# Cross-attention on one core: the output projection's quarters spread over the batches

## The chip, the cores and the metric

The kernel runs on one core of one Trainium2 chip. The metric is device time in microseconds (us) of one execution, lower is better. The core has a matrix engine (TensorE, PE in the rows, with its weight loads as PEld), VectorE (DVE), ScalarE (ACT), GpSimd (POOL) and SyncE (SP), which here only issues DMAs. Each runs its own instruction queue in order, and they wait for each other by semaphores.

## What is computed

32 batches of 56 queries attend to 1500 context rows each, with 32 heads of 16 dimensions. The context serves as keys and as values. Cut to what matters, the reference is:

```python
x = layernorm(hidden) * ln_gamma + ln_beta          # hidden: 32 x 56 x 512
Q = split_heads(x @ Wq.T)                            # 32 heads of 16
K = V = split_heads(ctx)                             # 32 x 1500 x 512
scores = einsum('bhsd,bhtd->bhst', Q, K) / 4
probs = softmax(where(mask, scores, -inf))
attn = einsum('bhst,bhtd->bhsd', probs, V).transpose(0, 2, 1, 3).reshape(B, S, 512)
return hidden + attn @ Wout.T
```

## The kernel before

The layer norm and the query projection of all batches come first (about the first 100 us). Then the main loop runs over 32 batches, and in each over 12 slots of 125 context rows. Slot k of a batch is one round of an attention pipeline, written out by hand on every engine.

- TensorE lays the negated row maxima into four PSUM banks (L266, `begin_scores`), adds the scores of all heads (L274, `score_blocks`), and later multiplies the slot before's exponentials with the values (L289, `times_values`). The four score banks are not doubled: L266 of slot k+1 waits for ScalarE's exponential of slot k.
- ScalarE takes the exponential of the whole slot in one instruction (L370, 125 x 1792 elements). There is one of them per slot, so its starts are the clock by which this document measures: slot k's length is the time from its start to that of slot k+1.
- To have the row maxima before the scores, TensorE also computes bfloat16 scores of a batch ahead: 48 tiles a batch, four a slot (L234, `score_tile`). VectorE adds the mask to each and takes its maximum (L335). These tiles pass through a ring of two PSUM banks: a tile may be written when the one two places before it in the ring has been taken. In a slot the first tile stands before L266; here it is called the lead tile. The second and third stand behind the scores, and the fourth behind the values.
- GpSimd adds the exponentials of every four slots (L422), and TensorE sums those over the context rows with a matrix of ones (L303, `add_denominators`). It does this in slots 6 and 7, 10 and 11, and in 2 and 3 of the next batch. VectorE inverts the sums in four reciprocals, one in slot 3 and three in slot 4 (`INVERT_AT`, L359), and GpSimd divides the heads by them (L435, `divide_heads`) into `attnT`, behind the third of its additions.
- Slot 10 also turns the maxima of the next batch (L242), for which VectorE first reduces them (L344).
- Two batches make a pair with 112 query rows. When the second batch of a pair is divided, the output projection of the pair is due: `project_out` (L251), in four quarters of 128 columns. Each quarter is a unit of the same ring of two PSUM banks; VectorE adds the residual (L352, `add_residual`) into `result`, from `x_res`, which SyncE loads (L208) before and stores (L212) after.

`OUT_AT` names where the quarters stand, as (batch of the pair after, slot). Each stands at the end of its slot, behind the fourth tile and ahead of the next slot's lead tile:

```python
OUT_AT = [(0, 8), (0, 9), (1, 0), (1, 1)]
```

The two engines' ends of the loop over slots read, on TensorE and on VectorE:

```python
                    if tiles:
                        score_tile(pe, tiles[3])
                    for unit in slot_others(b, k):
                        project_out(pe, unit)
```

So before the change a pair's quarters stand in slots 8 and 9 of the next even batch, and 0 and 1 of the odd batch behind it. `result`, `x_res` and `attnT` exist once each. The last pair's four quarters stand behind the loop.

Of the kernel before, what the change touches and what calls it, by code (L numbers as in the profile page):

```python
# [20 lines left out]
PAIR_Q = 2 * QUERIES  # L21
# [11 lines left out]
ROWS_SLOT = 10  # L33
OUT_PARTS = 4
OUT_COLS = HIDDEN // OUT_PARTS
OUT_AT = [(0, 8), (0, 9), (1, 0), (1, 1)]
TOKENS = BATCH * QUERIES

UNIT_TILES = [1, 3, 4, 4, 4]
# [15 lines left out]

def slot_others(b, k):

    return [("out", b // 2 - 1, OUT_AT.index((b % 2, k)))] if (b % 2, k) in OUT_AT and b > 1 else []

FIRST_TILES = [("tile", 0, t) for t in range(MAX_TILES)] + [("tile", 1, t) for t in range(AHEAD)]
RING = FIRST_TILES[:]
RING += [unit for b in range(BATCH) for k in range(SLOTS) for unit in slot_tiles(b, k) + slot_others(b, k)]
RING += [("out", BATCH // 2 - 1, part) for part in range(OUT_PARTS)]
RING_AT = {unit: n for n, unit in enumerate(RING)}


def build(nc, x, kt, ctx, mask_lanes, mask_rows, wq_t, wout_t, gamma, beta, out):
    with ExitStack() as stack:  # L70
        def sb(name, shape, dt=F32):
            return stack.enter_context(nc.sbuf_tensor(name, shape, dt))
# [20 lines left out]
        den_inv = sb("den_inv", [128, BLOCKS, QUERIES])  # L93
        own = sb("own", [128, 2, BLOCKS, QUERIES])
        heads = sb("heads", [128, BLOCKS, QUERIES])
        attnT = sb("attnT", [128, BLOCKS, PAIR_Q])
        x_res = sb("x_res", [128, HIDDEN])
        result = sb("result", [128, HIDDEN])
        ident = sb("ident", [128, 128])
# [80 lines left out]
        def filled_past(unit):  # L180
            return RING_AT[unit] + 1
# [63 lines left out]
        def project_out(pe, unit):  # L245

            _, d, part = unit
            bank = ring_bank(pe, unit)
            pe.wait_ge(attn_ready, 2 * d + 2)
            for g in range(BLOCKS):  # L250
                mm = nc.tensor.matmul(bank[0:PAIR_Q, 0:OUT_COLS], attnT[:, g, :],  # L251
                                      woutT[:, g, OUT_COLS * part:OUT_COLS * (part + 1)],
                                      start=(g == 0), stop=(g == BLOCKS - 1))
            mm.then_inc(ring_filled, 1)
# [68 lines left out]
        def take_unit(dve, unit):  # L323
            dve.wait_ge(ring_filled, filled_past(unit))
            if unit[0] == "tile":
                take_tile(dve, unit[1], unit[2], bank_of(unit))
            else:
                add_residual(dve, unit[1], unit[2], bank_of(unit))
# [99 lines left out]

        def divide_heads(pool, b):
            pool.wait_ge(den_taken, BLOCKS * (b + 1))  # L430
            if b % 2 == 0 and b > 0:
                pool.wait_ge(ring_filled, filled_past(("out", b // 2 - 1, OUT_PARTS - 1)))
            pool.wait_ge(heads_added, b + 1)
            at = QUERIES * (b % 2)
            nc.gpsimd.tensor_tensor(attnT[:, :, at:at + QUERIES], heads[:], den_inv[:], ALU.mult).then_inc(attn_ready, 1)  # L435

        end = BATCH - 1
        block = stack.enter_context(nc.Block())
# [2 lines left out]
        def _(sp):  # L441
# [30 lines left out]
            for b in range(BATCH):  # L472
                if b > 0:
                    if b < end:
                        sp.wait_ge(pv_done, SLOTS * b)
                        load_k(sp, b + 1, 2)
                    sp.wait_ge(pv_done, SLOTS * b)
                    load_v(sp, b, 2)
                if b < end:
                    sp.wait_ge(pv_done, SLOTS * b + CHUNK)  # L480
                    if b + 2 < BATCH:
                        load_k(sp, b + 2, 0)
                    load_v(sp, b + 1, 0)
                    if b + 2 < BATCH:
                        wait_taken(sp, ("tile", b, MAX_TILES - 1))
                        load_mask(sp, b + 2)
                if b % 2 == 1:
                    if b > 1:
                        store_result(sp, b // 2 - 1)
                    load_residual(sp, b // 2)  # L490
                if b + 2 < BATCH:
                    sp.wait_ge(pv_done, SLOTS * b + 2 * CHUNK)
                    load_k(sp, b + 2, 1)
                if b < end:
                    sp.wait_ge(pv_done, SLOTS * b + 2 * CHUNK)
# [54 lines left out]
        def _(dve):  # L550
# [52 lines left out]
                        take_unit(dve, unit)  # L603
            for g in range(BLOCKS):
                invert_denominators(dve, end, g)
            for part in range(OUT_PARTS):
                take_unit(dve, ("out", BATCH // 2 - 1, part))

        @block.scalar
        def _(act):  # L610
# [32 lines left out]
        def _(pe):  # L643
# [58 lines left out]
            pe.wait_ge(exped, BATCH * SLOTS)  # L702
            times_values(pe, end, SLOTS - 1)
            last_denominators(pe)
            for part in range(OUT_PARTS):
                project_out(pe, ("out", BATCH // 2 - 1, part))

# [41 lines left out]
```

## Time and profile before

| what | us |
|---|---|
| median of 3 runs (lowest, highest) | 1474.55 (1472.51, 1477.33) |
| the profiled execution: its time | 1475.04 |
| the profiled execution: its span, first to last instruction | 1473.3 |
| TensorE matmuls busy in the span | 1391.1 (94%) |
| GpSimd busy | 1242.8 (84%) |
| VectorE busy | 1072.2 (73%) |
| ScalarE busy | 751.6 (51%) |

A busy share is an average over all slots and says what an engine does, not who waits for whom. The mean granted TensorE clock is 0.992 of full speed. The rows further down are read by the start times of one kind of instruction, or by who stands behind whom inside a single slot.

### The profile page before, as it was taken

Reading aid. Unit: us, or ns where it says so; the run is one execution under the profiler, and the core shown is the slowest. Engines: PE = TensorE matmul, PEld = TensorE weight load, DVE = VectorE, ACT = ScalarE, POOL = GpSimd, SP = SyncE. Lnnn points to the kernel's source line nnn. Section 1 sums busy time; section 2 is a strip of 40 time slices with the busy share of each in tenths; the row PEclk is TensorE's granted clock in tenths of the full one; section 3 lists DMA queues with packets and bytes.
Section 4 is the critical chain, followed back from the end, with each engine's and each line's share of the span. In section 5 each row is a group of like instructions: output and inputs, shape, how many; then the busy total and the mean of one; then the engine's idle time right before and its main releaser. Section 6 shows DMA issues by size and latency. Waiting matters only on the chain.

```text
span 1473.3 us, 66063 instructions
## 1 busy us (share of the span) xinstructions
PE 1391.1 (94%) x30000; PEld 992.9 (67%) x30000; DVE 1072.2 (73%) x3356; ACT 751.6 (51%) x623; POOL 1242.8 (84%) x434
## 2 busy tenths in 40 slices
PE   6999999999999999999999999999999999999986
PEld 4337677676766767676676767676676767677675
DVE  6657777777777777777777777777777777777730
ACT  2125555555555555545555555554555555555553
POOL 1009998989999898989989898998989899898986
PEclk9999999999999999999999999999999999999999
DMA  9303444435444443444444444444344443444320
GB/s 296 80 38 141 176 165 146 171 135 183 158 166 166 148 171 141 174 161 156 176 164 152 155 156 166 172 151 166 149 160 158 162 171 148 175 159 152 147 86 8
DMA packets 39161, 224.90 MB, mean 153 GB/s; under 512 B 4546, under 2 KB 4578, under 8 KB 26882
## 3 DMA queue, kind: packets, MB, share of 16 engines
q1 hardware_dynamic: 38882, 220.68, 41.3%
q8 instruction: 236, 3.87, 1.1%
q14 instruction: 43, 0.35, 0.1%
HBM read 216.90 MB, written 3.77 MB: 150 GB/s over the span
## 4 chain that ended last, share of the span: by engine, by line
PE 68%; DVE 24%; ACT 4%; issue 3%; POOL 1%; DMA 0%; ACTq 0%; SPq 0%; POOLq 0%; DVEq 0%
PE ps L234 20%; DVE masked L335 18%; PE ps L289 17%; PE ps L274 12%; PE ps L303 6%; PE ps L251 5%; PE ps L266 4%; PE ps L664 4%; ACT probs L370 3%; DVE den_inv L359 3%; PE ps L242 1%; POOL sums L422 1%; DVE tile_max L335 1%; DVE stats L555 0%; DVE probs L572 0%
## 5 line engine op out<-in xcount | busy, mean ns | idle before, releaser
L335 DVE CUSTOM_DVE_ANT_0 masked<-ps,mask_tile 112x500 bf16<-112x500 f32 x1536 | 974.9, 672 | 310.1 <-PE ps L234 295.5
L370 ACT ACTIVATE probs<-ps,mask_bias 125x1792 f32<-125x1792 f32 x384 | 674.2, 1756 | 629.3 <-PE ps L274 607.1
L422 POOL TENSOR_TENSOR sums<-sums,probs 125x1792 f32<-125x1792 f32 x191 | 763.5, 3997 | 10.1
L422 POOL TENSOR_TENSOR sums<-probs 125x1792 f32<-125x1792 f32 x96 | 383.7, 3997 | 197.3 <-ACT probs L370 197.3
L234 PE MATMUL ps<-kT,qdb 32*112 32x500 bf16 x1536 | 487.7, 414 | 43.8 <-DVE tile_max L335 41.4
L274 PEld LDWEIGHTS ps<-qd,kT 32*125 32x125 f32 x12288 | 433.9, 185 | 1.6 <-issue 0.3
L274 PE MATMUL ps<-qd,kT 32*125 32x112 f32 x12288 | 432.7, 269 | 2.4 <-issue 2.4
L289 PE MATMUL ps<-probs,v 125*32 125x112 f32 x12288 | 372.9, 262 | 1.2 <-ACT probs L370 0.7
L289 PEld LDWEIGHTS ps<-probs,v 125*32 125x32 f32 x12288 | 299.2, 110 | 68.7 <-issue 44.8
L234 PEld LDWEIGHTS ps<-kT,qdb 32*112 32x112 bf16 x1536 | 157.9, 123 | 245.6 <-DVE tile_max L335 184.0
L266 PE MATMUL ps<-max_rows,ones_row 4*125 4x448 bf16 x1536 | 189.6, 389 | 12.7 <-ACT probs L370 9.8
L335 DVE DVE_READ_ACCUMULATOR2_ANT tile_max<- 112x1 f32 x1536 | 128.0, 83 | 0.0
L303 PE MATMUL ps<-sums,ones 125*32 125x224 f32 x1520 | 111.3, 365 | 0.0
L266 PEld LDWEIGHTS ps<-max_rows,ones_row 4*125 4x125 bf16 x1536 | 60.1, 129 | 53.8 <-ACT probs L370 38.2
L359 DVE RECIPROCAL den_inv<-ps 128x56 f32<-128x56 f32 x128 | 63.5, 500 | 34.2 <-PE ps L316 29.4
L251 PE MATMUL ps<-woutT,attnT 128*112 128x128 f32 x512 | 73.0, 288 | 5.0 <-POOL attnT L435 2.6
L251 PEld LDWEIGHTS ps<-woutT,attnT 128*112 128x112 f32 x512 | 60.8, 181 | 21.2 <-DVE tile_max L335 11.4
L664 PE MATMUL ps<-sums,v 128*128 128x448 f32 (+2 forms) x160 | 65.7, 530 | 3.1 <-DMA v<-in_wq_t 1.4
L303 PEld LDWEIGHTS ps<-sums,ones 125*32 125x32 f32 x1520 | 29.9, 108 | 43.0 <-issue 42.1
L352 DVE TENSOR_TENSOR result<-ps,x_res 112x128 f32<-112x128 f32 x64 | 18.7, 292 | 43.6 <-PE ps L251 43.6
L626 ACT COPY qT<-ps 128x448 f32<-128x448 f32 (+2 forms) x20 | 9.1, 457 | 63.5 <-PE ps L664 63.4
L664 PEld LDWEIGHTS ps<-sums,v 128*128 128x128 f32 x160 | 27.1, 212 | 18.8 <-issue 12.5
(49 smaller groups left out, 254.6 us busy)
## 6 DMA issues: line engine op xcount, KB each, us to landing
kT<-in_kt SPq DMA_DIRECT2D x96, 1000.0 KB, 5.2
v<-in_ctx SPq DMA_DIRECT2D x96, 1000.0 KB
mask_tile<-mask_add SPq DMA_DIRECT2D x32, 328.1 KB, 13.6
x_res<-in_x SPq DMA_DIRECT2D x16, 224.0 KB, 14.1
out<-result SPq DMA_DIRECT2D x16, 224.0 KB, 14.1
probs<-in_x SPq DMA_DIRECT2D x14, 224.0 KB, 9.2
v<-in_wq_t SPq DMA_DIRECT2D x1, 1024.0 KB, 5.9
woutT<-in_wout_t SPq DMA_DIRECT2D x1, 1024.0 KB, 20.7
```

The lines of the kernel that those rows point to most:

```text
L234: nc.tensor.matmul(bank[0:PAIR_Q, 0:KEYS], qdb[rows, b % 2, g, :], keys, start=True, stop=True).then_inc(ring_filled, 1)
L251: mm = nc.tensor.matmul(bank[0:PAIR_Q, 0:OUT_COLS], attnT[:, g, :], woutT[:, g, OUT_COLS * part:OUT_COLS * (part + 1)], start=(g == 0), st ...
L266: nc.tensor.matmul(ps[0:LANES, r, 0:BANK_Q], ones_row[rows, :], max_rows[rows, b % 2].rearrange("p g n -> p (g n)"), start=True, stop=Fals ...
L274: mm = nc.tensor.matmul(ps[0:LANES, r, PAIR_Q * g:PAIR_Q * (g + 1)], kT[rows, b % 2, k // CHUNK, g, k % CHUNK, :], qd[rows, b % 2, g, :], ...
L289: mm = nc.tensor.matmul(acc[ROW * r:ROW * (r + 1), g, :], v[0:LANES, c, k % CHUNK, col:col + ROW], probs[0:LANES, k % PROBS, r, PAIR_Q * g ...
L303: mm = nc.tensor.matmul(den[ROW * r:ROW * (r + 1), :, :], ones[0:LANES, e, :], own_q, start=(j == 0 and e == 0), stop=(j == SUMS - 1 and e ...
L335: nc.vector.tensor_tensor_reduce(out=masked[0:PAIR_Q, t % 2, :], in0=bank[0:PAIR_Q, 0:KEYS], in1=mask_tile[0:PAIR_Q, b % 2, KEYS * c:KEYS ...
L352: nc.vector.tensor_tensor(result[0:PAIR_Q, cols], bank[0:PAIR_Q, 0:OUT_COLS], x_res[0:PAIR_Q, cols], ALU.add).then_inc(ring_taken, 1)
L359: nc.vector.reciprocal(den_inv[:, g], den[:, g]).then_inc(den_taken, 1)
L370: nc.scalar.activation(probs[0:LANES, k % PROBS], ps[0:LANES, 0:TILES_R, 0:BANK_Q], ACT.Exp, bias=mask_bias[0:LANES, n:n + 1], scale=SCALE ...
L422: nc.gpsimd.tensor_tensor(total, before, probs[0:LANES, slot % PROBS], ALU.add).then_inc(summed, 1)
L664: mm = nc.tensor.matmul(bank, wqT[:, h, 128 * c:128 * (c + 1)], xT[u % 2][:, h, 0:w], start=(h == 0), stop=(h == BLOCKS - 1))
```

## The change

A pair's quarters move to (batch of the pair after, slot) (0, 9), (1, 3), (1, 9) and (2, 3), so that every batch from 3 on has one in slot 3 and one in slot 9. They now reach into the batches in which the next pair is divided, so `attnT` is doubled. SyncE's store of `result` and load of `x_res` move from the odd batches to the even ones. Of the last two pairs five quarters are left behind the loop, not four, and among them the store of the last pair but one and the load of the last residual. The diff, without what only follows from the new index of `attnT`:

```diff
-OUT_AT = [(0, 8), (0, 9), (1, 0), (1, 1)]
+OUT_AT = [(2, 9), (3, 3), (3, 9), (4, 3)]
...
 def slot_others(b, k):
-    return [("out", b // 2 - 1, OUT_AT.index((b % 2, k)))] if (b % 2, k) in OUT_AT and b > 1 else []
+    return [("out", (b - after) // 2, part) for part, (after, slot) in enumerate(OUT_AT)
+            if slot == k and after % 2 == b % 2 and b >= after]
...
-RING += [("out", BATCH // 2 - 1, part) for part in range(OUT_PARTS)]
+LAST_OUTS = [("out", d, part) for d in range(BATCH // 2 - 2, BATCH // 2) for part in range(OUT_PARTS)]
+LAST_OUTS = [unit for unit in LAST_OUTS if unit not in RING]
+RING += LAST_OUTS
...
-        attnT = sb("attnT", [128, BLOCKS, PAIR_Q])
+        attnT = sb("attnT", [128, 2, BLOCKS, PAIR_Q])
...
-            if b % 2 == 0 and b > 0:
-                pool.wait_ge(ring_filled, filled_past(("out", b // 2 - 1, OUT_PARTS - 1)))
+            if b % 2 == 0 and b > 2:
+                pool.wait_ge(ring_filled, filled_past(("out", b // 2 - 2, OUT_PARTS - 1)))
...
-                if b % 2 == 1:
-                    if b > 1:
-                        store_result(sp, b // 2 - 1)
-                    load_residual(sp, b // 2)
+                if b % 2 == 0:
+                    if b > 2:
+                        store_result(sp, b // 2 - 2)
+                    if b > 0:
+                        load_residual(sp, b // 2 - 1)
...
+            store_result(sp, BATCH // 2 - 2)
+            load_residual(sp, BATCH // 2 - 1)
             store_result(sp, BATCH // 2 - 1)
```

TensorE before the change, batch 2, from the values of slot 8 to the start of slot 10's scores (L234 is a tile, L251 a quarter, L289 the values, L266 and L274 the next slot's scores):

```order
L289 MATMUL ps<-probs,v 32x112 x16
L234 MATMUL ps<-kT,qdb 112x500
L251 MATMUL ps<-woutT,attnT 112x128 x4
L234 MATMUL ps<-kT,qdb 112x500
L266 MATMUL ps<-max_rows,ones_row 125x448 x4
L274 MATMUL ps<-qd,kT 125x112 x16
L234 MATMUL ps<-kT,qdb 112x500 x2
L289 MATMUL ps<-probs,v 32x112 x16
L234 MATMUL ps<-kT,qdb 112x500
L251 MATMUL ps<-woutT,attnT 112x128 x4
L234 MATMUL ps<-kT,qdb 112x500
L266 MATMUL ps<-max_rows,ones_row 125x448 x4
```

TensorE after the change, the same place (the line numbers are 3 higher):

```order
L292 MATMUL ps<-probs,v 32x112 x16
L237 MATMUL ps<-kT,qdb 112x500 x2
L269 MATMUL ps<-max_rows,ones_row 125x448 x4
L277 MATMUL ps<-qd,kT 125x112 x16
L237 MATMUL ps<-kT,qdb 112x500 x2
L292 MATMUL ps<-probs,v 32x112 x16
L237 MATMUL ps<-kT,qdb 112x500
L254 MATMUL ps<-woutT,attnT 112x128 x4
L237 MATMUL ps<-kT,qdb 112x500
L269 MATMUL ps<-max_rows,ones_row 125x448 x4
L277 MATMUL ps<-qd,kT 125x112 x16
L237 MATMUL ps<-kT,qdb 112x500 x2
```

The quarter of slot 8 is gone, and that of slot 9 stands where it stood.

VectorE before the change, batch 3, from the end of slot 3's last tile to the middle of slot 4 (L335 a tile in two instructions, L359 a reciprocal):

```order
L335 ISA tile_max 112x1
L359 RECIPROCAL den_inv<-ps 128x56
L335 ISA masked,tile_max<-ps,mask_tile 112x500
L335 ISA tile_max 112x1
L359 RECIPROCAL den_inv<-ps 128x56
L335 ISA masked,tile_max<-ps,mask_tile 112x500
L335 ISA tile_max 112x1
L335 ISA masked,tile_max<-ps,mask_tile 112x500
L335 ISA tile_max 112x1
L359 RECIPROCAL den_inv<-ps 128x56
```

VectorE after the change, the same place:

```order
L338 ISA tile_max 112x1
L362 RECIPROCAL den_inv<-ps 128x56
L355 TENSOR_TENSOR result<-ps,x_res 112x128
L338 ISA masked,tile_max<-ps,mask_tile 112x500
L338 ISA tile_max 112x1
L362 RECIPROCAL den_inv<-ps 128x56
L338 ISA masked,tile_max<-ps,mask_tile 112x500
L338 ISA tile_max 112x1
L338 ISA masked,tile_max<-ps,mask_tile 112x500
L338 ISA tile_max 112x1
L362 RECIPROCAL den_inv<-ps 128x56
```

The residual addition of a quarter now stands between slot 3's reciprocal and slot 4's lead tile. On TensorE the quarter stands in slot 3 in the same way, behind the fourth tile.

SyncE before the change, an even batch from its slot 4 on and the odd one behind it up to its slot 4:

```order
L195 DMA kT<-in_kt 128x2000
L199 DMA v<-in_ctx 125x2048
L202 DMA mask_tile<-mask_add 112x1500
L195 DMA kT<-in_kt 128x2000
L199 DMA v<-in_ctx 125x2048
L195 DMA kT<-in_kt 128x2000
L199 DMA v<-in_ctx 125x2048
L195 DMA kT<-in_kt 128x2000
L199 DMA v<-in_ctx 125x2048
L202 DMA mask_tile<-mask_add 112x1500
L212 DMA out<-result 112x512
L208 DMA x_res<-in_x 112x512
```

SyncE after the change, the same place:

```order
L198 DMA kT<-in_kt 128x2000
L202 DMA v<-in_ctx 125x2048
L205 DMA mask_tile<-mask_add 112x1500
L215 DMA out<-result 112x512
L211 DMA x_res<-in_x 112x512
L198 DMA kT<-in_kt 128x2000
L202 DMA v<-in_ctx 125x2048
L198 DMA kT<-in_kt 128x2000
L202 DMA v<-in_ctx 125x2048
L198 DMA kT<-in_kt 128x2000
L202 DMA v<-in_ctx 125x2048
L205 DMA mask_tile<-mask_add 112x1500
```

The store and the load of the residual moved from behind the mask of the odd batch to behind that of the even batch.

## Rows read from the trace of the kernel before

Times are us from the span's start. A row of a timeline is start, duration, engine, line, operation, tiles, count, and in brackets the idle time ahead of it with what ended it.

**Rows 1.** The page, part 4: the chain that ended last, by engine.
```profile
PE 68%; DVE 24%; ACT 4%; issue 3%; POOL 1%; DMA 0%; ACTq 0%; SPq 0%; POOLq 0%; DVEq 0%
```

**Rows 2.** Timeline of ScalarE, batches 13 and 14: start, duration, line, tiles, wait.
```profile
654.61 1.75 ACT L370 ACTIVATE probs<-ps,mask_bias 125x1792 f32<-125x1792 f32 x1 [1.68 <-PE ps L274]
...
663.10 1.76 ACT L370 ACTIVATE probs<-ps,mask_bias 125x1792 f32<-125x1792 f32 x1 [2.27 <-PE ps L274]
...
669.65 1.76 ACT L370 ACTIVATE probs<-ps,mask_bias 125x1792 f32<-125x1792 f32 x1 [1.56 <-PE ps L274]
...
683.14 1.76 ACT L370 ACTIVATE probs<-ps,mask_bias 125x1792 f32<-125x1792 f32 x1 [1.68 <-PE ps L274]
...
689.62 1.75 ACT L370 ACTIVATE probs<-ps,mask_bias 125x1792 f32<-125x1792 f32 x1 [1.48 <-PE ps L274]
...
697.17 1.76 ACT L370 ACTIVATE probs<-ps,mask_bias 125x1792 f32<-125x1792 f32 x1 [1.68 <-PE ps L274]
...
706.88 1.75 ACT L370 ACTIVATE probs<-ps,mask_bias 125x1792 f32<-125x1792 f32 x1 [1.48 <-PE ps L274]
710.20 1.75 ACT L370 ACTIVATE probs<-ps,mask_bias 125x1792 f32<-125x1792 f32 x1 [1.56 <-PE ps L274]
713.87 1.75 ACT L370 ACTIVATE probs<-ps,mask_bias 125x1792 f32<-125x1792 f32 x1 [1.92 <-PE ps L274]
...
723.93 1.76 ACT L370 ACTIVATE probs<-ps,mask_bias 125x1792 f32<-125x1792 f32 x1 [1.68 <-PE ps L274]
728.39 1.76 ACT L370 ACTIVATE probs<-ps,mask_bias 125x1792 f32<-125x1792 f32 x1 [2.71 <-PE ps L274]
732.42 1.76 ACT L370 ACTIVATE probs<-ps,mask_bias 125x1792 f32<-125x1792 f32 x1 [2.27 <-PE ps L274]
...
739.46 1.76 ACT L370 ACTIVATE probs<-ps,mask_bias 125x1792 f32<-125x1792 f32 x1 [1.68 <-PE ps L274]
```

**Rows 3.** Timeline of TensorE, batch 14, slot 8 into 9 and 10.
```profile
725.33 0.42 PE L234 MATMUL ps<-kT,qdb 32*112 32x500 bf16 x1
725.69 1.13 PE L251 MATMUL ps<-woutT,attnT 128*112 128x128 f32 x8
726.74 0.42 PE L234 MATMUL ps<-kT,qdb 32*112 32x500 bf16 x1
...
729.20 0.42 PE L234 MATMUL ps<-kT,qdb 32*112 32x500 bf16 x1
...
732.20 0.42 PE L234 MATMUL ps<-kT,qdb 32*112 32x500 bf16 x1
```

**Rows 4.** Timeline of TensorE, batch 13, slot 9 and start of slot 10.
```profile
687.61 0.69 PE L234 MATMUL ps<-kT,qdb 32*112 32x500 bf16 x2
...
689.91 0.42 PE L234 MATMUL ps<-kT,qdb 32*112 32x500 bf16 x1 [0.24 <-DVE tile_max L335]
```

**Rows 5.** Timeline of TensorE, batch 14, end of slot 3, start of 4.
```profile
708.51 0.42 PE L234 MATMUL ps<-kT,qdb 32*112 32x500 bf16 x2
...
710.67 0.42 PE L234 MATMUL ps<-kT,qdb 32*112 32x500 bf16 x1 [0.40 <-DVE tile_max L335]
```

**Rows 6.** Timeline of the SyncE queue, batch 14, slot 4.
```profile
712.82 0.44 SPq L202 DMA_DIRECT2D mask_tile<-mask_add  x1
```

**Rows 7.** DMA times to landing by tile: of x_res.
```profile
DMA to landing us min/median/max: 6.3/14.1/14.8
```

**Rows 8.** The same of out (from result).
```profile
DMA to landing us min/median/max: 2.3/14.1/14.5
```

**Rows 9.** Timeline of all engines, batch 31 and the end.
```profile
1432.91 0.41 PE L266 MATMUL ps<-max_rows,ones_row 4*125 4x448 bf16 x4 [0.78 <-ACT probs L370]
...
1464.12 0.66 POOL L435 TENSOR_TENSOR attnT<-heads,den_inv 128x224 f32<-128x224 f32 x1 [2.61 <-DVE den_inv L359]
...
1464.92 5.39 PE L251 MATMUL ps<-woutT,attnT 128*112 128x128 f32 x32 [2.61 <-POOL attnT L435]
```

**Rows 10.** Windows at the end: busy us (instructions) by engine, granted clock, DMA.
```profile
1466.00:1470.00 4.00, 4.00 (x24) 4.00 (x24) 0.88 (x3) 0.00 (x0) 0.00 (x0) 0.60 0.01 4
```

More of the change, by code:

```diff
@@ L250, in project_out @@
             for g in range(BLOCKS):
-                mm = nc.tensor.matmul(bank[0:PAIR_Q, 0:OUT_COLS], attnT[:, g, :],
+                mm = nc.tensor.matmul(bank[0:PAIR_Q, 0:OUT_COLS], attnT[:, d % 2, g, :],
                                       woutT[:, g, OUT_COLS * part:OUT_COLS * (part + 1)],
@@ L430, in divide_heads @@
             pool.wait_ge(den_taken, BLOCKS * (b + 1))
-            if b % 2 == 0 and b > 0:
-                pool.wait_ge(ring_filled, filled_past(("out", b // 2 - 1, OUT_PARTS - 1)))
+            if b % 2 == 0 and b > 2:
+                pool.wait_ge(ring_filled, filled_past(("out", b // 2 - 2, OUT_PARTS - 1)))
             pool.wait_ge(heads_added, b + 1)
             at = QUERIES * (b % 2)
-            nc.gpsimd.tensor_tensor(attnT[:, :, at:at + QUERIES], heads[:], den_inv[:], ALU.mult).then_inc(attn_ready, 1)
+            nc.gpsimd.tensor_tensor(attnT[:, b // 2 % 2, :, at:at + QUERIES], heads[:], den_inv[:], ALU.mult).then_inc(attn_ready, 1)
         end = BATCH - 1
@@ L605, in _ @@
                 invert_denominators(dve, end, g)
-            for part in range(OUT_PARTS):
-                take_unit(dve, ("out", BATCH // 2 - 1, part))
+            for unit in LAST_OUTS:
+                take_unit(dve, unit)
         @block.scalar
@@ L704, in _ @@
             last_denominators(pe)
-            for part in range(OUT_PARTS):
-                project_out(pe, ("out", BATCH // 2 - 1, part))
+            for unit in LAST_OUTS:
+                project_out(pe, unit)
 FILL_PLAN = [(kind, 0, c) for kind in ("x", "q") for c in range(BLOCKS)] + [("x", 1, c) for c in range(BLOCKS)]
```

## The prediction

> **What bounds the kernel now.** I read the chain that ended last first: 68% of it is TensorE, 24% VectorE, nothing on GpSimd or DMA that counts [rows 1]. TensorE is thus the engine to follow, but a share does not say what one more instruction costs in a given slot. For that I took the starts of the exponentials, one per slot, over an odd and an even batch in a row [rows 2]. Batch 13 lasts 697.17 - 654.61 = 42.56 us and batch 14 739.46 - 697.17 = 42.29, a pair 84.85.
>
> The reader is to see three kinds of slot in [rows 2]. Slots 0 to 2 of batch 14 take 9.71 together, 3.24 each, and so do batch 13's slots 8 and 9 (6.48). There an exponential takes 1.76, the next scores start behind it and need the other 1.48 (the bracket): the loop of ScalarE and the scores sets the pace, and TensorE has a little room. Slots with more TensorE work are longer: slot 3 takes 3.32. And a slot with a quarter takes 4.46 (batch 14, slot 8, 723.93 to 728.39), the next one with a quarter 4.03. In batch 13 slots 0 and 1 take 8.49, the same two costs.
>
> Inside such a slot the fourth tile starts at 725.33, the quarter at 725.69, the next lead tile at 726.74 [rows 3]: 1.41 from fourth tile to lead tile, and 728.39 - 726.74 = 1.65 more to the next exponential. Without a quarter the fourth and the lead tile start together [rows 5]. That gives me the rule that I use below: with a quarter, slot length = start of the fourth tile after the exponential + 1.41 + 1.65. For slot 8: 1.40 + 3.06 = 4.46.
>
> The last thing to see is what a quarter leaves behind. While TensorE does it, VectorE runs out of tiles and catches up. In slot 9 behind a quarter the fourth tile starts 0.81 after the exponential (729.20 - 728.39 [rows 2, 3]), in the ordinary slot 9 of batch 13 1.23 after (687.61, with the exponential 3.24 before 689.62 [rows 2, 4]). And in slot 10 the third tile starts 0.22 before the exponential when slot 9 had a quarter (732.20 against 732.42), but 0.29 after it, held by VectorE, when it had none (689.91 against 689.62 [rows 2 to 4]). The credit is worth 0.51: slots 10 and 11 take 7.04 in batch 14 and 7.55 in batch 13.
>
> **The change slot by slot.** Nothing is computed more or less: 64 quarters and 64 residual additions before and after. What changes is in which slot they fall, and what VectorE's rest is good for there.
>
> Slot 9, now in every batch, alone: fourth tile at 1.23, so 1.23 + 3.06 = 4.29. Against batch 13's 3.24 that is a cost of 1.05; against batch 14's 4.03 it is 0.26 more, since there the quarter before had paid for it. Its credit in slot 10 stays in even batches and is new in odd ones (-0.51).
>
> Slots 8, 0 and 1: the quarters leave. Slot 8 falls to 3.24 (-1.22 in even batches), slots 0 and 1 to 6.47 (-2.02 in odd ones). Slots 2 and 3 of batch 13 took 6.55 and those of batch 14 6.56, so the leaving itself takes nothing back there.
>
> Slot 3, now in every batch: the fourth tile starts at 708.51 - 706.88 = 1.63 [rows 2, 5], late already, because the denominators stand in this slot. With the quarter: 1.63 + 3.06 = 4.69, a cost of 1.37. This is the dear place. The credit comes in slot 4: there the third tile waits 0.40 for VectorE and starts 0.47 after the exponential [rows 5], since the reciprocal of slot 3 and the first of slot 4 stand ahead of it. With the quarter, the reciprocal of slot 3 runs beside it, and the third tile finds its bank free as in slot 9 behind a quarter. Slot 4 then is an ordinary 3.24 where it was 713.87 - 710.20 = 3.67. Slots 5 to 7 took 10.06 in batch 14, 0.35 over three ordinary ones, since VectorE enters them behind the other two reciprocals and TensorE meets its backlog in the denominator slots. It now enters a little earlier; I take 9.92, nearer to the row than to 9.71, so 13.16 for slots 4 to 7. They took 13.73 in batch 14 and 13.49 in batch 13 [rows 2], where the quarters of slots 0 and 1 had left VectorE a little ahead. The bounds are 12.95 and, if nothing is given back, 13.73.
>
> The new batch: 9.71 + 4.69 + 13.16 + 3.24 + 4.29 + 7.04 = 42.13. An even batch gains 0.16, an odd one 0.43. Thirteen even batches (4 to 28) and fourteen odd ones (3 to 29) give 2.1 + 6.0 = 8.1. Batch 2 only loses its quarter of slot 8 and keeps slot 9: 42.29 - 1.22 + 0.26, a gain of 1.0. In batch 30 I count 0.2 gained, as in any even one. Batch 31 has no tiles, so TensorE waits 0.78 for the exponential in slot 3 [rows 9] and a quarter of 1.13 [rows 3] costs 0.35 there; slot 9's is hidden, as slots 0 and 1 were. Together 9.0 gained in the loop.
>
> **Waits that move.** GpSimd's first exponential sum of a batch still waits for slot 1, and its third, behind which `attnT` is made, is done by slot 5; both `attnT` halves are free by then. SyncE issues the store and the residual load behind the mask, whose issue is at 712.82, 2.62 after slot 4's exponential [rows 2, 6]. After the change the values stand about 0.9 earlier in slot 4, so the mask goes out at 1.7, the store at 2.1, the load at 2.6 after it. The quarter of slot 9 is added some 2.7 after slot 9's exponential, which is 13.16 + 3.24 = 16.4 later than slot 4's. So the load has 16.5 us. It takes 14.1, at most 14.8 [rows 7], and the store 14.5 at most [rows 8]. Hidden, with 1.7 to spare. If that cover fails, VectorE waits in slot 9 with the lead tile of slot 10 queued behind it, and TensorE's third tile behind that.
>
> **The end.** Of five quarters the first needs only old heads: it runs between the last denominators and the division, a gap in which TensorE idles 2.61 [rows 9]; 1.13 fits. But its addition stands behind the last reciprocals (about 1464.1), so SyncE issues the store at about 1464.4 and the last residual at 1464.8. The additions wait for it, where before the first could run when its quarter was done, at 1464.92 + 1.13 = 1466.05 [rows 3, 9]. The landing costs between 2.3 (the last store, with nothing beside it [rows 8]) and 6.3 (the fastest residual [rows 7]). With 2.3 it is there at 1467.1, and the third quarter starts on its bank at 1467.4, when TensorE is still at the second: nothing lost. With 6.3 it is there at 1471.1, then two more quarters of 1.1 follow, some 3 us lost. The queue is empty as for the last store, so I take 2.8, and a loss of 0.3.
>
> The Trainium skill (DMA: Bandwidth & Descriptors, Anatomy of one DMA) gives about 2.0 us fixed and the bytes over 436 GB/s, though for GpSimd's path: an estimate of 2.5 us for 224 KB, near the lower row, and no loss at the end. No run here shows that path.
>
> Sum against the profiled execution: 1475.0 - 9.0 + 0.3 = 1466.3. It lies 0.5 above the median of the runs shown, so for the median I say 1465.8.
>
> **Rivals.** *Slot 10's credit fails in odd batches* (take_max stands between the residual addition and slot 10's lead tile; a lone quarter in slot 9 adds 0.26 later than the second of two). Then 14 x 0.51 = 7.1 is missing: 1472.9, about no change. For it: no row shows a lone quarter in slot 9. Against: its lead tile is later by the same 0.26.
>
> *Slot 3 gives nothing back* (the other side). The quarter puts its residual addition between two reciprocals, and VectorE's backlog stays: slots 4 to 7 take 13.73. The batch is 42.70; even batches lose 0.41 x 13, odd ones 0.14 x 14, together 7.3; batch 2 still gains 1.0, batches 30 and 31 and the end lose 1.1: 1474.55 + 7.4 = 1482. It decides from 13.47 for these four slots (8.9 over 28 batches is 0.31 each), where the gain is gone. Against it: the addition waits only for the quarter, and slot 4's wait of 0.40 is for tiles that the quarter lets VectorE finish.
>
> *The residual comes late.* A landing of over 16.5 costs its excess once a pair; 14 pairs at 1 us are 14 us, but the rows leave 1.7 us. At 17.2 the time is 1475.6.
>
> *The clock at the end.* In the last quarters the granted clock is 0.60 [rows 10], between the levels 1.2 and 2.4 GHz, after TensorE had idled twice. The extra quarter fills part of the second gap; if the clock stays full, at most 4.0 x 0.4 = 1.6 is saved: 1464.2. The Trainium skill (TensorE: Matmul & The Clock Gate, What's actually happening) has the throttled state as the default that activity releases, which speaks for it; whether so short a filling does it, no row here shows.
>
> **How the numbers follow.** My forecast 0.66; the clock beside it 0.08; slot 10's credit missing 0.14; slot 3 without credit 0.08; a late residual 0.04. Runs of one kernel lie some 2.5 us around their median, so 0.3% (4.4 us) is what can be told from no change. Faster: 0.66 + 0.08 = 0.74 and a little of the partial cases, 0.75. Slower 0.09, the rest 0.16. The range takes in the clock, slot 10's case and that spread: 1461 to 1473.5.
>
> **What would show it.** After: slots 3 at 4.69, 4 at 3.24, 8 at 3.24, 9 at 4.29 and 10 with 11 at 7.04 in both kinds of batch; batches of 42.1; no wait of VectorE's residual addition for a DMA but the first one at the end. Wrong would be a slot 4 of over 3.4, a slot 10 of 4.1 in odd batches, a wait for x_res in slot 9.

## The result and the profile after

The changed kernel takes 1465.68 us (median of 5 runs, 1463.32 to 1466.77) where the kernel before took 1472.57 beside it (5 runs, 1471.99 to 1477.33). The ratio is 0.9942, with a 95% interval of 0.9929 to 0.9955: faster by 0.6%. A later comparison on another chip, with 6 and 11 runs, gave 0.9931 (0.9915 to 0.9946).

The page's chain that ended last, by engine, answers to [rows 1]: VectorE's share fell from 24% to 10%, TensorE's rose to 81%.

```profile
PE 81%; DVE 10%; ACT 6%; issue 1%; DMA 1%; POOL 1%; ACTq 0%; SPq 0%; DVEq 0%; POOLq 0%
```

The timeline of ScalarE in batch 14 (start, duration, line, tiles, wait) answers to [rows 2]. Its rows start slots 0, 3, 4, 5, 8, 9, 10 and the next batch's slot 0.

```profile
693.73 1.76 ACT L373 ACTIVATE probs<-ps,mask_bias 125x1792 f32<-125x1792 f32 x1 [1.68 <-PE ps L277]
...
703.44 1.75 ACT L373 ACTIVATE probs<-ps,mask_bias 125x1792 f32<-125x1792 f32 x1 [1.48 <-PE ps L277]
708.11 1.76 ACT L373 ACTIVATE probs<-ps,mask_bias 125x1792 f32<-125x1792 f32 x1 [2.92 <-PE ps L277]
711.35 1.75 ACT L373 ACTIVATE probs<-ps,mask_bias 125x1792 f32<-125x1792 f32 x1 [1.48 <-PE ps L277]
...
721.14 1.75 ACT L373 ACTIVATE probs<-ps,mask_bias 125x1792 f32<-125x1792 f32 x1 [1.56 <-PE ps L277]
724.38 1.75 ACT L373 ACTIVATE probs<-ps,mask_bias 125x1792 f32<-125x1792 f32 x1 [1.48 <-PE ps L277]
728.65 1.76 ACT L373 ACTIVATE probs<-ps,mask_bias 125x1792 f32<-125x1792 f32 x1 [2.52 <-PE ps L277]
...
735.69 1.76 ACT L373 ACTIVATE probs<-ps,mask_bias 125x1792 f32<-125x1792 f32 x1 [1.68 <-PE ps L277]
```

The reader is to see a slot 3 of 4.67 (703.44 to 708.11), a slot 4 of 3.24, slots 5 to 7 in 9.79, slot 8 in 3.24, slot 9 in 4.27, slots 10 and 11 in 7.04, and a batch of 41.96 where it was 42.29. Fifteen of the 27 batches from 3 to 29 read so, odd and even. Batches 4, 8, up to 28 are longer by the slot 5 that the last section describes, and others by a slot 6 or 7 in which TensorE stands still.

The timeline of VectorE, TensorE and SyncE in slot 4 of the same batch answers to [rows 5, 6]. Its last row is VectorE's residual addition in slot 9:

```profile
707.53 0.50 DVE L362 RECIPROCAL den_inv<-ps 128x56 f32<-128x56 f32 x1
...
707.68 0.41 PE L237 MATMUL ps<-kT,qdb 32*112 32x500 bf16 x1
...
709.29 0.50 DVE L362 RECIPROCAL den_inv<-ps 128x56 f32<-128x56 f32 x1
...
710.25 0.50 DVE L362 RECIPROCAL den_inv<-ps 128x56 f32<-128x56 f32 x1
...
711.10 0.44 SPq L211 DMA_DIRECT2D x_res<-in_x  x1
...
727.11 0.29 DVE L355 TENSOR_TENSOR result<-ps,x_res 112x128 f32<-112x128 f32 x1 [0.37 <-PE ps L254]
```

The third tile starts at 707.68, 0.43 ahead of the exponential at 708.11, and is held by nothing; before, it started 0.47 behind it. The three reciprocals of slot 4 are where they were, but slot 4 takes 3.24 in spite of them.

The end, in the timeline of all engines, answers to [rows 9]:

```profile
1450.70 1.13 PE L254 MATMUL ps<-woutT,attnT 128*112 128x128 f32 x8
...
1452.58 0.66 POOL L438 TENSOR_TENSOR attnT<-heads,den_inv 128x224 f32<-128x224 f32 x1 [2.62 <-DVE den_inv L362]
...
1453.05 0.43 SPq L211 DMA_DIRECT2D x_res<-in_x  x1
...
1453.38 1.97 PE L254 MATMUL ps<-woutT,attnT 128*112 128x128 f32 x16 [1.55 <-POOL attnT L438]
1456.24 0.49 DVE L355 TENSOR_TENSOR result<-ps,x_res 112x128 f32<-112x128 f32 x2 [3.59 <-DMA x_res<-in_x]
...
1456.58 2.00 PE L254 MATMUL ps<-woutT,attnT 128*112 128x128 f32 x16 [1.24 <-DVE result L355]
```

The windows there (span, busy us of TensorE, its weight loads, VectorE, ScalarE and GpSimd, each with instructions; granted clock; DMA share; GB/s) answer to [rows 10]:

```profile
1452.00:1456.00 4.00, 1.97 (x16) 1.80 (x16) 0.64 (x3) 0.00 (x0) 0.66 (x1) 1.00 0.39 119
1456.00:1460.00 4.00, 2.00 (x16) 1.80 (x16) 1.07 (x4) 0.00 (x0) 0.00 (x0) 1.00 0.05 15
```

And the residual's times to landing answer to [rows 7]:

```profile
DMA to landing us min/median/max: 3.1/14.3/15.1
```

### The profile page after: what moved, and what is told of

Read it like the earlier page. It is cut to its first block, busy times and chain, and to the rows that moved or that the text cites. A ratio compares the mean times of both kernels' runs of the same rounds, so it can differ in the third digit from the quotient of the medians.

```text
span 1461.6 us, 66063 instructions
## 1 busy us (share of the span) xinstructions
PE 1404.7 (96%) x30000; PEld 992.2 (68%) x30000; DVE 1079.4 (74%) x3356; ACT 750.7 (51%) x623; POOL 1243.8 (85%) x434
## 3 DMA queue, kind: packets, MB, share of 16 engines
q8 instruction: 236, 3.87, 1.1%
## 4 chain that ended last, share of the span: by engine, by line
PE 81%; DVE 10%; ACT 6%; issue 1%; DMA 1%; POOL 1%; ACTq 0%; SPq 0%; DVEq 0%; POOLq 0%
PE ps L237 23%; PE ps L292 19%; PE ps L277 17%; DVE masked L338 9%; PE ps L306 6%; PE ps L269 6%; ACT probs L373 6%; PE ps L254 4%; PE ps L670 4%; PE ps L245 1%; POOL sums L425 1%; DMA v<-in_wq_t 0%; DVE probs L578 0%; DVE den_inv L362 0%; PE ps L661 0%
## 5 line engine op out<-in xcount | busy, mean ns | idle before, releaser
L277 PEld LDWEIGHTS ps<-qd,kT 32*125 32x125 f32 x12288 | 423.7, 184 | 1.9 <-issue 0.9
L277 PE MATMUL ps<-qd,kT 32*125 32x112 f32 x12288 | 421.4, 268 | 0.8 <-issue 0.6
L237 PEld LDWEIGHTS ps<-kT,qdb 32*112 32x112 bf16 x1536 | 161.3, 123 | 217.2 <-DVE tile_max L338 151.2
L269 PE MATMUL ps<-max_rows,ones_row 4*125 4x448 bf16 x1536 | 179.6, 392 | 14.3 <-ACT probs L373 11.1
```

The costliest lines, as they stand in the source:

```text
L237: nc.tensor.matmul(bank[0:PAIR_Q, 0:KEYS], qdb[rows, b % 2, g, :], keys, start=True, stop=True).then_inc(ring_filled, 1)
L269: nc.tensor.matmul(ps[0:LANES, r, 0:BANK_Q], ones_row[rows, :], max_rows[rows, b % 2].rearrange("p g n -> p (g n)"), start=True, stop=Fals ...
L277: mm = nc.tensor.matmul(ps[0:LANES, r, PAIR_Q * g:PAIR_Q * (g + 1)], kT[rows, b % 2, k // CHUNK, g, k % CHUNK, :], qd[rows, b % 2, g, :], ...
```

## The experiments

All are compared with the kernel before, run beside them on the same chip. Its median there was 1472.57 for the changed kernel, 1474.51 for pairs_kept and the three kernels named slots, 1474.97 for busy_slot_3, busy_slot_9, residual_late and two_results, and 1475.11 for the other four. Line numbers are those of each kernel. Slot lengths are medians over batches 4 to 29, from the starts of the exponentials in each one's trace; where even and odd batches differ only by the 3.51 described at the end, the odd ones are given. The column "batch" is their sum. In changed_again and two_results slot 9 takes 4.14 and not 4.27 in most even batches; there too the odd ones are given.

| kernel | slots with a quarter | batch | median us | ratio (95%) |
|---|---|---|---|---|
| before | 8 9 / 0 1 | 42.28 / 42.55 | 1472.57 | |
| changed | 9 and 3 | 41.97 | 1465.68 | 0.9942 (0.9929, 0.9955) |
| changed_again | 9 and 3 | 41.97 | 1465.16 | 0.9931 (0.9915, 0.9946) |
| pairs_kept | 0 1 / 8 9 | 42.55 / 42.27 | 1474.70 | 1.0003 (0.9995, 1.0012) |
| slots_8_and_1 | 8 and 1 | 42.40 | 1475.88 | 1.0005 (0.9993, 1.0017) |
| slots_8_and_3 | 8 and 3 | 42.25 | 1472.38 | 0.9999 (0.9980, 1.0017) |
| slots_9_and_1 | 9 and 1 | 42.12 | 1466.49 | 0.9946 (0.9931, 0.9960) |
| busy_slot_3 | 9 and 3 | 42.23 | 1470.01 | 0.9971 (0.9958, 0.9984) |
| busy_slot_9 | 9 and 3 | 42.23 | 1470.04 | 0.9964 (0.9952, 0.9976) |
| busy_three | 9 and 3 | 43.21 | 1493.78 | 1.0127 (1.0105, 1.0150) |
| residual_late | 8 and 3 | see text | 1481.00 | 1.0044 (1.0029, 1.0059) |
| two_results | 9 and 3 | 41.97 | 1463.11 | 0.9917 (0.9902, 0.9933) |
| early_recips_9_and_3 | 9 and 3 | 41.84 | 1459.08 | 0.9893 (0.9876, 0.9910) |
| early_recips_9_and_1 | 9 and 1 | 41.52 | 1450.22 | 0.9832 (0.9815, 0.9848) |

**Which slots, or the held heads?** The changed kernel with its quarters side by side again:

```diff
-OUT_AT = [(2, 9), (3, 3), (3, 9), (4, 3)]
+OUT_AT = [(3, 8), (3, 9), (4, 0), (4, 1)]
```

> The whole changed kernel (two halves of attnT, store and load of the residual in even batches), but the quarters stand in neighbouring slots again, 8 and 9 of odd batches and 0 and 1 of even ones. My theory, that the gain is in which slots the quarters stand: batches of 42.3 and 42.55 as before, slots of 4.46 and 4.02 with a quarter; the time is the kernel's before less 2 us, since two quarters more stand behind the loop, ratio 0.9985. Rival, that the held heads or the moved DMAs bring the gain: batches of 42.0, ratio 0.994.

The batches are those of before, with even and odd exchanged. Its timeline of ScalarE in batch 14, slots 0 and 1:

```profile
696.85 1.75 ACT L373 ACTIVATE probs<-ps,mask_bias 125x1792 f32<-125x1792 f32 x1 [1.68 <-PE ps L277]
...
701.31 1.75 ACT L373 ACTIVATE probs<-ps,mask_bias 125x1792 f32<-125x1792 f32 x1 [2.03 <-PE ps L277]
705.33 1.76 ACT L373 ACTIVATE probs<-ps,mask_bias 125x1792 f32<-125x1792 f32 x1 [2.27 <-PE ps L277]
```

4.46 and 4.02, as before. So holding the heads and moving the DMAs brings nothing. The 2 us that I expected from the two quarters more behind the loop did not come: the last exponential starts 2.5 earlier (at 1454.57, before at 1457.06), but from there to the end of the span it takes 17.6 where it took 16.2, and the 0.9985 expected lies outside the interval of the ratio.

**Any spreading?** One quarter at a time, elsewhere. In slots_8_and_1 and slots_8_and_3 the store and the load of the residual go ahead of slot 4's other DMAs:

```diff
-OUT_AT = [(2, 9), (3, 3), (3, 9), (4, 3)]
+OUT_AT = [(2, 8), (3, 1), (3, 8), (4, 1)]      # slots_8_and_1
+OUT_AT = [(2, 9), (3, 1), (3, 9), (4, 1)]      # slots_9_and_1
+OUT_AT = [(2, 8), (3, 3), (3, 8), (4, 3)]      # slots_8_and_3
...
                     sp.wait_ge(pv_done, SLOTS * b + CHUNK)
+                    if b % 2 == 0:
+                        if b > 2:
+                            store_result(sp, b // 2 - 2)
+                        if b > 0:
+                            load_residual(sp, b // 2 - 1)
                     if b + 2 < BATCH:
                         load_k(sp, b + 2, 0)
```

> Quarters spread as in the change, one at a time, but in slots 8 and 1 of each batch; the residual's store and load stand ahead of the other DMAs of slot 4, so that they land in time. My theory, that a place is worth what the slot can give back: slot 8 costs 1.22 and slot 1 1.05, slot 4 stays 3.44, slot 10 gets most of its credit through slot 9; a batch of 42.4, no gain, ratio 1.000 (with 0.1 either way). Rival, that spreading the quarters is what counts wherever they stand: a batch of 42.0, ratio 0.994.

> Slot 9 as in the change, slot 1 in place of 3. My theory: slot 1 costs 1.05 and gives back 0.23 in slot 4 (3.44), slot 3 is 3.32, slots 5 to 7 take 10.06; a batch of 42.15 against 41.97, 5 us more than the changed kernel, ratio to before 0.998. If slot 3 had no part in the gain: as the changed kernel or better, ratio 0.994 or less, since slot 1 has room that slot 3 lacks.

> Slot 3 as in the change, slot 8 in place of 9; the residual's store and load stand ahead of the other DMAs of slot 4. My theory: slot 8 is 4.46, slot 9 3.24, slots 10 and 11 7.1; a batch of 42.25, 8 us more than the changed kernel, ratio to before 1.000. If slot 9 had no part in the gain: ratio 0.994.

The timeline of ScalarE in batch 15 of slots_8_and_1 (slots 1, 2, 4, 8, 9, 10 and the next 0):

```profile
744.52 1.75 ACT L373 ACTIVATE probs<-ps,mask_bias 125x1792 f32<-125x1792 f32 x1 [0.81 <-PE ps L277]
748.81 1.75 ACT L373 ACTIVATE probs<-ps,mask_bias 125x1792 f32<-125x1792 f32 x1 [2.54 <-PE ps L277]
...
755.36 1.75 ACT L373 ACTIVATE probs<-ps,mask_bias 125x1792 f32<-125x1792 f32 x1 [1.56 <-PE ps L277]
...
768.85 1.76 ACT L373 ACTIVATE probs<-ps,mask_bias 125x1792 f32<-125x1792 f32 x1 [1.68 <-POOL sums L425]
773.32 1.75 ACT L373 ACTIVATE probs<-ps,mask_bias 125x1792 f32<-125x1792 f32 x1 [2.71 <-PE ps L277]
776.55 1.76 ACT L373 ACTIVATE probs<-ps,mask_bias 125x1792 f32<-125x1792 f32 x1 [1.48 <-PE ps L277]
...
783.69 1.75 ACT L373 ACTIVATE probs<-ps,mask_bias 125x1792 f32<-125x1792 f32 x1 [1.68 <-PE ps L277]
```

Slot 1 takes 4.29, slots 4 to 7 13.49, slot 8 4.47, slots 10 and 11 7.14. Spread like this, the quarters gain nothing. The batches of all three came out within 0.03 of what was expected, and slot 9 in place of 8 is worth 0.28 a batch. The DMAs that stand elsewhere do not blur this: slots 3 to 7 of slots_8_and_3 are those of the changed kernel (4.68, 3.24, 9.79). Slot 3 in place of 1 is worth 0.15 a batch in the slots, but the runs do not tell slots_9_and_1 from the changed kernel; my 0.998 was too high.

**VectorE's rest?** The changed kernel with idle reciprocals on VectorE, ahead of the residual addition:

```diff
+                    if (k, n) == (3, 3) and b > 2:     # (9, 3) in busy_slot_9; both, range(3), in busy_three
+                        for i in range(2):
+                            nc.vector.reciprocal(spare[:, 2 * (b % 2) + i], woutT[:, 0, 0:QUERIES])
                     for unit in slot_others(b, k):
                         take_unit(dve, unit)
```

> The changed kernel with two reciprocals more on VectorE in slot 3, between slot 3's reciprocal and the residual addition; they write to a tile that nothing reads and feed nothing. VectorE is busy three quarters of the time, so there is room on average. My theory, that slot 3's quarter gives back because VectorE catches up beside it: the 0.8 to 1.0 us take that rest away, slot 4 goes from 3.24 back to about 3.67 and slots 5 to 7 from 9.79 to 10.06; 0.7 a batch, 19 us more than the changed kernel, ratio to before 1.007. Rival, that the gain is TensorE's alone (an order of matmuls that costs less): slot 4 stays at 3.24, ratio 0.994.

> The same two reciprocals in slot 9, between its last tile and the residual addition. My theory: slot 9 stays at 4.28, slots 10 and 11 go from 7.05 back to about 7.55, as in the odd batches of before; 14 us more than the changed kernel, ratio to before 1.004. Rival, that slot 10 is shorter for another reason than VectorE's rest: 7.05, ratio 0.994.

> The changed kernel with three idle reciprocals (0.445 each) in slot 3 and three in slot 9, ahead of the residual addition; they feed nothing. With two, slot 4 kept its 3.24 with the third tile at 0.02 behind the exponential (-0.43 without them), slots 5 to 7 lost 0.26 and slot 10 lost 0.25 of 0.51. My theory, VectorE's rest: each further reciprocal moves the third tile by its whole 0.445. Slot 4's goes to 0.47, as in batch 14 of before, and the slot to 3.67; slot 10's goes from 0.04 to 0.49 and the slot from 3.86 to 4.31. A batch of 43.35, 38 us more than the changed kernel, ratio to before 1.020. Rival, that the credit lost with two was all that VectorE has to do with it: slot 4 stays at 3.24, slot 10 at 3.86, ratio 0.999.

With two, part of the credit went: slot 4 kept 3.24 but slots 5 to 7 went from 9.79 to 10.05, and slot 10 from 3.61 to 3.86. I had sized it too large: the two take 0.8, but slot 4's lead tile is taken only 0.48 later, and the third tile then starts 0.02 behind the exponential, where TensorE still waits for ScalarE. So the ratios came out at 0.9971 and 0.9964 where I expected 1.007 and 1.004. With three, the rest of it goes. The timeline of busy_three, batch 15: the three idle reciprocals, and slot 4's third tile.

```profile
761.61 1.17 DVE L612 RECIPROCAL spare<-woutT 128x56 f32<-128x56 f32 x3
...
763.56 0.12 PEld L238 LDWEIGHTS ps<-kT,qdb 32*112 32x112 bf16 x1 [0.47 <-DVE tile_max L339]
```

The timeline of its ScalarE, slot 4:

```profile
763.18 1.75 ACT L374 ACTIVATE probs<-ps,mask_bias 125x1792 f32<-125x1792 f32 x1 [2.92 <-PE ps L278]
766.77 1.75 ACT L374 ACTIVATE probs<-ps,mask_bias 125x1792 f32<-125x1792 f32 x1 [1.83 <-PE ps L278]
```

The third tile starts 0.38 behind the exponential, held by VectorE, and slot 4 takes 3.59 of the 3.67 of before. Slot 10 takes 4.23, over the 4.12 of before's odd batches. The three take 1.17 together, 0.36 for each but the first, where I had counted 0.445; that is why both stay 0.08 short of what was expected. The ratio, 1.0127, is short of the expected 1.020 by more than that. VectorE is busy 74% of the span in the changed kernel, yet 1.17 us more in each of two slots a batch cost 28.6 us, 2%, on the same chip (1493.78 for 1465.16). That the credit is VectorE's rest is thus shown, for both places.

**A late residual.** slots_8_and_3 with the store and load behind the mask again, where the changed kernel has them:

```diff
-OUT_AT = [(2, 9), (3, 3), (3, 9), (4, 3)]
+OUT_AT = [(2, 8), (3, 3), (3, 8), (4, 3)]
```

> Quarters in slots 8 and 3, with the residual's store and load behind the mask as in the change. From its issue (2.6 behind slot 4's exponential) to its use in slot 8 the residual has 13.3 us and needs 14.1 to 14.8. My theory: VectorE waits for it in slot 8 of even batches, which goes from 4.45 to 5.3 or 5.9; 12 to 20 us more than with quarters in slots 8 and 3 and an early load, ratio to before 1.009 to 1.014. Rival, that such a wait is absorbed by VectorE's idle time: ratio 1.000.

VectorE's waits, longest first (us in total, times, longest):

```profile
DVE result L355 <- DMA x_res<-in_x: 18.2, 13, 3.3
```

The longest, 3.3, is the one at the end, which slots_8_and_3 has too. The other twelve stand in slot 8 of even batches, 0.8 to 1.9 each and 14.9 together. The quarter's own slot does not grow (4.15 to 4.46 in even batches, as with the early load). The cost comes behind it: the median slot 10 of even batches is 4.13 (3.70 with the early load), and in the four batches with waits of 1.6 or more slot 9 takes 3.5 to 3.9 and not 3.24. Slots 8 to 11 of batches 2 to 28, the even ones, take 8.3 more together than in slots_8_and_3; the two ratios differ by 0.0045, 6.6 us. So both theories were half right: the wait is there, and about half of it is absorbed, by the rest that VectorE has after a quarter.

**The end.** Two tiles of `x_res` and `result`, with the last residual loaded at the start of batch 31:

```diff
-        x_res = sb("x_res", [128, HIDDEN])
-        result = sb("result", [128, HIDDEN])
+        x_res = sb("x_res", [128, 2, HIDDEN])
+        result = sb("result", [128, 2, HIDDEN])
...
+                if b == end:
+                    load_residual(sp, BATCH // 2 - 1)
```

> The changed kernel with x_res and result doubled, and the last residual loaded at the start of batch 31, so that nothing at the end waits for a load. The loop stays as it is (a batch of 41.97). At the end the first addition of the last pair no longer waits 3.6 for the load: from the last attnT to the last instruction 7.4 in place of 9.0 if the granted clock stays full; if it falls as in the kernel before, 9 or more. About 1.5 us less than the changed kernel, ratio to before 0.993.

The timeline of its end:

```profile
1454.15 0.66 POOL L438 TENSOR_TENSOR attnT<-heads,den_inv 128x224 f32<-128x224 f32 x1 [2.63 <-DVE den_inv L362]
...
1454.95 3.72 PE L254 MATMUL ps<-woutT,attnT 128*112 128x128 f32 x32 [1.55 <-POOL attnT L438]
1456.09 0.29 DVE L355 TENSOR_TENSOR result<-ps,x_res 112x128 f32<-112x128 f32 x1 [1.87 <-PE ps L254]
```

From the last `attnT` (1454.15) to the span's end (1461.7) it takes 7.5, where the changed kernel took 9.0 (1452.58 to 1461.6) and the kernel before 9.2 [rows 9]. The ratio, 0.9917, is near the 0.993 expected, but its interval overlaps that of the changed kernel.

**Without the backlog, which slot?** two_results with all reciprocals where VectorE waits for a tile anyway, with quarters in 9 and 3 or in 9 and 1. Two of the four move: the first stands one tile earlier, the last one tile later.

```diff
-INVERT_AT = [(3, 3), (4, 0), (4, 2), (4, 3)]
+INVERT_AT = [(3, 2), (4, 0), (4, 2), (5, 0)]
```

> The changed kernel with two residual and result tiles, and the four reciprocals moved to places where VectorE waits for a tile: behind the third tile of slot 3, the lead and third tiles of slot 4 and the lead tile of slot 5. My theory: slot 3's quarter had already given VectorE the time for them, so nothing is left to win: slot 4 3.24, slots 5 to 7 9.79, a batch of 41.97, ratio to before 0.992 as with two result tiles alone. Rival, that reciprocals hold VectorE up with a quarter beside them too: less than 41.9.

> The same, with quarters in slots 9 and 1. My theory: once the reciprocals cost no slot anything, slot 3's quarter has nothing to give back, and slot 1 is the cheaper place (fourth tile at 1.23 and not 1.62): slot 1 4.28, slot 3 3.32 or less, slot 4 3.24, slots 5 to 7 9.79; a batch of 41.65, 9 us less than with quarters in 9 and 3, ratio to before 0.986. Rival, that the backlog in slots 4 to 7 has another source than where the reciprocals stand: slot 4 3.44, slots 5 to 7 10.06, a batch of 42.1, ratio 0.993.

> The changed kernel once more, beside the others on one chip: a batch of 41.97, ratio 0.9942 within its interval.

The timeline of ScalarE in early_recips_9_and_1, batch 15 (slots 0, 1, 2, 4, 8, 9, 10 and the next 0):

```profile
730.12 1.76 ACT L373 ACTIVATE probs<-ps,mask_bias 125x1792 f32<-125x1792 f32 x1 [1.68 <-PE ps L277]
...
733.36 1.75 ACT L373 ACTIVATE probs<-ps,mask_bias 125x1792 f32<-125x1792 f32 x1 [0.81 <-PE ps L277]
737.64 1.76 ACT L373 ACTIVATE probs<-ps,mask_bias 125x1792 f32<-125x1792 f32 x1 [2.53 <-PE ps L277]
...
744.19 1.75 ACT L373 ACTIVATE probs<-ps,mask_bias 125x1792 f32<-125x1792 f32 x1 [1.56 <-PE ps L277]
...
757.22 1.75 ACT L373 ACTIVATE probs<-ps,mask_bias 125x1792 f32<-125x1792 f32 x1 [1.56 <-PE ps L277]
760.46 1.75 ACT L373 ACTIVATE probs<-ps,mask_bias 125x1792 f32<-125x1792 f32 x1 [1.48 <-PE ps L277]
764.60 1.76 ACT L373 ACTIVATE probs<-ps,mask_bias 125x1792 f32<-125x1792 f32 x1 [2.38 <-PE ps L277]
...
771.64 1.75 ACT L373 ACTIVATE probs<-ps,mask_bias 125x1792 f32<-125x1792 f32 x1 [1.68 <-PE ps L277]
```

Slot 1 takes 4.28, slots 4 to 7 13.03, slot 9 4.14, the batch 41.52. The order of the two places turned round, as the theory says: with the backlog slot 3 is the better by 0.15 a batch, without it slot 1 by 0.32. The rival of early_recips_9_and_3 was right in part: its batch is 41.84 and its ratio 0.9893, with the expected 0.992 outside the interval. Slot 9 takes 4.14 and not 4.27 in 23 of the 27 batches, where the changed kernel has 4.14 in 7 of them. That less of the backlog reached slot 8 is my reading; no run separates it. The last kernel is the best of all, 1.7% under the kernel before and, on one chip, 14.9 us under the changed one.

## Why the prediction was right

It said 1465.8 and 0.75 for faster. By its own steps:

- **The rule for a slot with a quarter** (fourth tile + 1.41 + 1.65) held: slot 3 4.67 for 4.69, slot 9 4.27 for 4.29, and in the experiments slot 8 4.46 and slot 1 4.28.
- **Slot 10's credit** was there for a lone quarter: 7.04 for slots 10 and 11 in odd batches too. The first rival fell. Taken together, the tables of slots give a quarter a net cost of 0.8 in slot 8 (1.22 less 0.42 in slot 10), 0.8 in slot 1 (1.04 less 0.23 in slot 4), 0.65 in slot 3 (1.35 less 0.43 and 0.27) and 0.5 in slot 9 (1.03 less 0.51); a batch without one would be 40.8, and the four kinds of batch with two lone quarters and the reciprocals of before (9 and 3, 9 and 1, 8 and 3, 8 and 1) are that sum to 0.03. Side by side they are dearer: slots 8 and 9 together cost 1.5 and not 1.3 (42.28), since only the second of them has the credit of slot 10.
- **Slot 4's credit** was there, 3.24; the slower rival fell. Slots 5 to 7 were mis-sized, 9.79 for 9.92, because the backlog had gone wholly and not in part; a batch is 41.97 for 42.13.
- **The moved DMAs** stayed hidden, with less to spare: the load is issued at 711.10, 2.99 behind the exponential and not 2.6, and used at 727.1; it has 16.0 and takes at most 15.1. The only wait of a residual addition for a DMA is the one at the end. residual_late shows that about half of a miss is absorbed.
- **The end** came out even (9.0 for 9.2) where I had a loss of 0.3. Two terms that I had not joined cancel: the additions wait 3.6 for the residual, which lands 3.2 from its issue where I took 2.8, and hold the third quarter for 1.24; and the fourth rival came true, the granted clock stayed at 1.00 and the last pair's quarters took 1.97 + 2.00 in place of 5.39. By the Trainium skill (TensorE: Matmul & The Clock Gate, What's actually happening) activity releases the throttle. These rows agree: all thirteen traces with one or two quarters in the gap keep 1.00 to the last quarter (3.72 for the four in two_results), and only the kernel before, whose gap is empty, falls to 0.60. With two quarters in the gap (pairs_kept) the clock holds even over a later idle time of 2.73. That the extra quarter in the gap is what keeps it is argued even so; no run took the quarter away alone.
- **The sum** is right partly by luck. From the ordinary slots one reads a gain of 0.31 x 13 + 0.58 x 14 = 12.2 us for batches 3 to 29, where I had 8.1. But in batches 4, 8, up to 28 slot 5 takes 3.51 in both kernels. Before, slots 6 and 7 were 0.26 shorter in these batches and the batch stayed 42.28; in the changed kernel they have nothing left to give, and such a batch is 42.24 by its ordinary slots. That takes back 7 x 0.27 = 1.9, a term that I had not seen. The two traces give 1149.5 - 1138.9 = 10.6 for batches 3 to 29, and with 1.0 for batch 2, 0.7 for batch 30 (I had 0.2) and a loss of 0.2 in batch 31 (I had 0.35) the loop gained 12.1 where I had 9.0. The medians of the runs give less, 6.9 in all, or 8.5 by the ratio, and 10 in the later comparison: the trace before is that of a run 2.5 above its median, the changed kernel's that of one 2.4 below. The excess of the 27 batches over the sum of their ordinary slots was 4.2 before, 5.7 in the changed kernel's trace and 8.4 in its second; 1.9 of the last two is the slot 5, and the rest is described in the last section.

## What to carry to other kernels

Where two engines take turns, ask of an inserted piece of work not only what it costs in its place but what the other engine does meanwhile, and what is late just behind: the same quarter cost 0.8 net in slot 8 or 1 and 0.5 in slot 9. In this kernel a good place for extra work on the bound engine was right ahead of where it would wait for the other's backlog; and once that backlog was gone (here by two reciprocals moved by one tile each), the better place was another, so place both together. Mean idle time says nothing on it: 1.17 us of work in each of two slots a batch, on an engine that is idle a quarter of the time, cost 2%.

## What was not expected of the hardware

**TensorE stands still in slots 6 and 7.** Its timeline in the kernel before, batch 21, slot 6, in the middle of the scores:

```profile
1018.09 1.16 PE L274 MATMUL ps<-qd,kT 32*125 32x112 f32 x31
...
1020.85 0.25 PE L274 MATMUL ps<-qd,kT 32*125 32x112 f32 x1 [1.60 <-issue]
```

The idle time is put down to "issue": the engine waited for nothing that the profile shows. Slots over 0.25 longer than their median (without the 3.51 below, and without residual_late) number 4 to 12 in a trace of batches 3 to 29, 80 of 91 in slots 6 and 7, some in the same batch of kernel after kernel: batch 12's slot 6 in ten of thirteen traces, batch 18's slot 7 in ten. The excess over ordinary slots, with those of 3.51, is 2 to 9 us a trace, and less in busy_three, the slowest kernel (2.0), than in the quickest (7.5).

What the engine waits for can be read from the DMA packets in the traces. The instruction queue (q8 on the page) moves 3.87 MB in 236 packets of 16 KB, one in 5.5 us on the median. Ahead of the standstill above there was none from 1008.9 to 1018.2, while data moved. The kernel before, DMA queues (packets, MB, share of 16 engines) from 1009 to 1018.1, with q8 absent, and from 1018.1 to 1020.8:

```profile
q1 hardware_dynamic: 430, 1.84, 62.9%
...
q8 instruction: 1, 0.02, 2.9%
```

The fourteen traces have 40 idle times of TensorE over 0.4 us in the loop that are put down to "issue". Every one ends 2.3 to 3.1 us after the start of a q8 packet that came late, 7.8 to 12.0 us after the one before it. Of 2286 packets that came within 7 us of the one before, none is followed by such an idle time; of 14 that came after 10 us or more, 10 are. 60000 of the 66063 instructions that the page counts are TensorE's. I take from this that TensorE waits there for its next instructions, though no run changed how they come. All 24 packets that came 9.5 us or more after the one before fall into slot 6, and slots 4 to 7 carry the batch's largest transfers; that these hold the packets up is argued, and moving slot 4's loads would test it.

A standstill can cost more than itself. The same trace, 1022 to 1025.5 (busy us of TensorE, its weight loads, VectorE, ScalarE and GpSimd; granted clock; DMA share; GB/s):

```profile
1022.00:1025.50 3.50, 3.50 (x64) 2.85 (x56) 1.88 (x6) 0.97 (x1) 3.50 (x3) 0.51 0.33 131
```

The granted clock is 0.51, at the 1.2 GHz level, and slot 7 is 1.04 longer. Four of the fourteen traces show such a stretch right behind an idle time (of 0.90, 1.35, 1.60 and 2.40 us); right behind others, of up to 1.53, the clock held. A fifth, slots_8_and_1, has a longer stretch, 10.2 us at 0.50 from 1330.6, behind an idle time of 0.68 in which TensorE waited for VectorE; slots 10 and 11 of its batch 28 are 4.8 longer.

**Slot 5 of every fourth batch** (4, 8, up to 28) takes 3.51 and not 3.24 in every kernel here, wherever the quarters are. The changed kernel's TensorE and ScalarE in slot 5 of batch 14, an ordinary one (from 711.35), and of batch 16 (from 795.27):

```profile
713.40 1.03 PE L277 MATMUL ps<-qd,kT 32*125 32x112 f32 x32
714.59 1.76 ACT L373 ACTIVATE probs<-ps,mask_bias 125x1792 f32<-125x1792 f32 x1 [1.48 <-PE ps L277]
...
797.32 1.03 PE L277 MATMUL ps<-qd,kT 32*125 32x112 f32 x32
798.78 1.75 ACT L373 ACTIVATE probs<-ps,mask_bias 125x1792 f32<-125x1792 f32 x1 [1.76 <-PE ps L277]
```

The scores start 2.05 after the exponential in both and take the same 1.03; it is ScalarE that starts 0.27 later behind them. Why it does is open.

**A reciprocal costs less behind another:** 1.17 for three where one alone shows 0.445.
